# Delta-rule blocks of 16x16 inverted on VectorE, one block per partition, instead of by doublings on TensorE

## The reference

```python
def step(Sm, inp):
    q_, k_, v_, g_, b_ = inp
    Sm = Sm * jnp.exp(g_)[..., None, None]
    kv = jnp.einsum('bhk,bhkv->bhv', k_, Sm)
    delta = (v_ - kv) * b_[..., None]
    Sm = Sm + jnp.einsum('bhk,bhv->bhkv', k_, delta)
    o = jnp.einsum('bhk,bhkv->bhv', q_, Sm)
    return (Sm, o)
```

## Time and profile before

| | |
|---|---|
| median of three runs | 2876.7 us (2873.14 to 2880.99) |
| span of the profiled execution | 2973.8 us, mean TensorE clock 0.954 of full |
| PE, PEld busy | 2684.9 us (90%), 2275.1 us (77%) |
| DVE busy | 2384.7 us (80%) |
| ACT, POOL busy | 1828.3 us (61%), 1221.2 us (41%) |
| DMA | 153.27 MB, mean 52 GB/s |

### The profile page before, as it was taken

How to read it: one execution, slowest core, us unless ns; L and a number is a source line. 1 busy time by engine, 2 the same in 40 slices (tenths; PEclk the granted TensorE clock), 3 DMA queues, 4 the chain that set the end, 5 groups by cost and what they waited for, 6 DMA issues and landing times. The chain is left out here.

```text
span 2973.8 us, 122804 instructions
## 1 busy us (share of the span) xinstructions
PE 2684.9 (90%) x52271; PEld 2275.1 (77%) x52272; DVE 2384.7 (80%) x5006; ACT 1828.3 (61%) x5749; POOL 1221.2 (41%) x1048
## 2 busy tenths in 40 slices
PE   1478889999999999999999999999999999857898
PEld 1367668888888888888888888888888888724555
DVE  7556658888888888888888888888888888468796
ACT  1245546777777777777777777777777777501111
POOL 2456555343434343434343434343434343255420
PEclk7778889999999999999999999999999999978999
DMA  5221101111111111111111111111111110152311
GB/s 189 92 61 42 32 23 38 35 42 35 42 35 42 35 42 35 42 36 41 39 42 41 39 39 42 41 40 37 42 35 42 35 32 28 61 192 90 94 64 43
DMA packets 92834, 153.27 MB, mean 52 GB/s; under 512 B 16966, under 2 KB 60661, under 8 KB 91107
## 3 DMA queue, kind: packets, MB, share of 16 engines
q1 hardware_dynamic: 69491, 111.65, 12.9%
q0 software_dynamic: 12288, 24.19, 2.6%
q10 hardware_dynamic: 10512, 9.57, 0.9%
HBM read 114.38 MB, written 40.37 MB: 52 GB/s over the span
## 5 line engine op out<-in xcount | busy, mean ns | idle before, releaser
L1383 DVE SCALAR_TENSOR_TENSOR p_y<-p_xr,cw,p_y 128x512 f32<-128x512 f32 x768 | 652.2, 851 | 66.7 <-ACT p_y L1101 46.6
L740 PE MATMUL p_psF<-xnS,w_hl 128*128 128x512 f32 x1536 | 432.8, 417 | 24.1 <-PEq L628 11.1
L1655 POOL TENSOR_TENSOR p_Wr<-p_Ws,p_rho 128x512 f32<-128x512 f32 x96 | 135.8, 1436 | 651.0 <-ACT p_Ws L1198 651.0
L740 PEld LDWEIGHTS p_psF<-xnS,w_hl 128*128 128x128 f32 x1536 | 279.3, 195 | 87.3 <-issue 18.2
L1637 POOL TENSOR_TENSOR p_E<-p_E,p_sj 128x512 f32<-128x512 f32 x128 | 158.0, 1253 | 292.9 <-DVE p_sj L1409 292.9
L800 PEld LDWEIGHTS p_psI<-p_Dc,p_M 32*32 32x32 f32 x16384 | 180.1, 106 | 100.0 <-issue 91.9
L922 PE MATMUL p_psO<-p_wout,p_ont 128*128 128x256 f32 x1024 | 250.4, 399 | 0.7 <-ACT p_ont L1211 0.7
L800 PE MATMUL p_psI<-p_Dc,p_M 32*32 32x32 f32 x16384 | 215.7, 195 | 38.1 <-issue 33.7
L1678 POOL TENSOR_TENSOR p_O<-p_OG,p_sm 128x512 f32<-128x512 f32 x128 | 131.4, 1049 | 240.9 <-DVE p_sm L58 240.8
L1098 ACT ACTIVATE p_xr<-p_psF 128x512 f32<-128x512 f32 x256 | 154.1, 602 | 123.0 <-PE p_psF L740 119.8
L810 PEld LDWEIGHTS p_psI<-p_Xs,p_DTc 32*32 32x32 f32 x16384 | 168.5, 106 | 75.0 <-issue 70.0
(11 more groups left out here) (322 smaller groups left out, 6638.8 us busy)
## 6 DMA issues: line engine op xcount, KB each, us to landing
p_ab<-decays SPq DMA_DIRECT2D x64, 512.0 KB
w_raw<-in_w_in SPq DMA_DIRECT2D x16, 768.0 KB, 5.6
p_wgu<-in_w_gu SPq DMA_DIRECT2D x60, 176.0 KB
expert_out<-p_ye ACTq DMA_DIRECT2D x73, 128.0 KB, 1.8
expert_in<-p_zero SPq DMA_DIRECT2D x16, 512.0 KB, 7.1
p_xe<-expert_in SPq DMA_DIRECT2D x60, 128.0 KB
p_wd<-in_w_down SPq DMA_DIRECT2D x60, 88.0 KB
p_wout<-in_w_out SPq DMA_DIRECT2D x16, 256.0 KB
```

What stands on the lines that cost most here:

```text
L740: m = pe.matmul(b4(psF[f % 2][:, :]), w_hl[:, wp, kt, ty * P:(ty + 1) * P], xnS[:, xp, kt, :].rearrange("p (b t) -> p b t", b=B)[:, :, c * ...
L1383: m = dve.scalar_tensor_tensor(y[:, ty, :, :], xr[:, ty, :, tap:tap + P], cw[:, ty, tap:tap + 1], y[:, ty, :, :], ALU.mult, ALU.add)
```

## The change

Levels 1 to 3 and first_level go, with their passes on TensorE, copies on ScalarE and masks on GpSimd. Instead, compact(g) writes the 32 x 32 blocks with the opposite sign, SyncE stores them to DRAM (blocks_out), and gathers the 64 diagonal blocks of 16 x 16 (2 value heads, 4 batches, 8 blocks each) into U, one block in a partition as 256 elements. pivots(g) on VectorE inverts them in place: for each of the pivots 1 to 14 it multiplies the column above the pivot with the row to its right and adds the product. SyncE writes the blocks back to DRAM (blocks_back, whose other places hold zeros), and loads the 32 x 32 blocks into DTc, and turn_cores transposes them into Dc. From there level 4 goes on as before, with the one mask that it needs, and adds where it subtracted. pivots(g - 1) stands where the VectorE part of level 1 stood, turn_cores(g - 1) where level 3 stood. compact(g) moves on ScalarE ahead of squares(g, 1). SyncE's loads of a step are issued one step earlier in its program, between the transfers back and those out. Some semaphores and constants are merged.

```diff
+            def cores_out(g):
+                wait(sp, "compact", g, 4)
+                sp.dma_start(block_rows(blocks_out), ATc[:, :, :, :].rearrange("p v b t -> p (v b t)")).then_inc(apart, 16)
+                sp.wait_ge(apart, 16 * (g + 1))
+                for s_ in range(2):
+                    at = slice(s_ * CORES // 2, (s_ + 1) * CORES // 2)
+                    sp.dma_start(U[at, 0:CORE * CORE], core_rows(blocks_out, s_)).then_inc(gathered, 16)
+            def cores_back(g):
...
+                wait(sp, "pivoted", g, 1)
+                for s_ in range(2):
+                    at = slice(s_ * CORES // 2, (s_ + 1) * CORES // 2)
+                    sp.dma_start(core_rows(blocks_back, s_), U[at, 0:CORE * CORE]).then_inc(returned, 16)
+                sp.wait_ge(returned, 16 + 32 * (g + 1))
+                wait(sp, "spread", g - 2, 4)
+                sp.dma_start(DTc[g % 2][:, :, :, :].rearrange("p v b t -> p (v b t)"), block_rows(blocks_back)).then_inc(inverted, 16)
             def step(g):
-                decays_in(g)
-                unit_in(g)
-                head_in(g)
+                cores_back(g - 1)
+                loads(g + 1)
+                cores_out(g)
+                if g + 1 < STEPS:
+                    head_in(g + 1)
...
-                wait(act, "masked", g - 1, 2)
-                wait_event(act, "inverse_d", 1, g - 1)
+                wait(act, "masked", g - 1, 1)
+                if g:
+                    act.wait_ge(apart, 16 * g)
                 for q in range(4):
-                    act.activation(heads(ATc[quad(q), :, :, :]), heads(ATP[g % 2][quad(q), :, :, 0, quad(q)]), ACT.Copy).then_inc(s["compact"], 1)
+                    act.activation(heads(ATc[quad(q), :, :, :]), heads(ATP[g % 2][quad(q), :, :, 0, quad(q)]), ACT.Copy, scale=-1.0).then_inc(s["compact"], 1)
...
+            def pivots(g):
+                dve.wait_ge(gathered, 32 * (g + 1))
+                mark(dve.memset(diagonal, 1.0))
+                for k in range(1, CORE - 1):
+                    n = CORE - 1 - k
+                    rest, product = square[:, 0:k, k + 1:], pivot[:, 0:k * n].rearrange("p (i j) -> p i j", i=k)
+                    link(dve.tensor_tensor(product, square[:, 0:k, k:k + 1].to_broadcast([CORES, k, n]), square[:, k:k + 1, k + 1:].to_broadcast([CORES, k, n]), ALU.mult))
+                    m = dve.tensor_tensor(rest, rest, product, ALU.add)
+                    if k < CORE - 2:
+                        link(m)
+                m.then_inc(s["pivoted"], 1)
+            def turn_cores(g):
                 p = g % 2
                 wait(dve, "halved", g - 2, 2)
-                wait(dve, "spread", g - 2, 4)
                 wait_event(dve, "inverse_mm", "x5", g - 2)
-                wait(dve, "compact", g, 4)
-                link(dve.tensor_tensor(heads(Dc[p][:, :, :, :]), heads(ATc[:, :, :, :]), masks[:, 0, :].unsqueeze(1).to_broadcast([P, 2 * B, BLK]), ALU.mult))
-                link(dve.tensor_tensor(heads(DTc[p][:, :, :, :]), identc[:, :].unsqueeze(1).to_broadcast([P, 2 * B, BLK]), heads(Dc[p][:, :, :, :]), ALU.subtract))
+                dve.wait_ge(inverted, 16 * (g + 1))
                 dve.transpose(heads(Dc[p][:, :, :, :]), heads(DTc[p][:, :, :, :])).then_inc(s["inverse_d"], 1)
...
                 if g >= 1:
-                    level(g - 1, 1)
+                    pivots(g - 1)
```

More of the change, by code:

```diff
@@ L370, in link @@
                 ch.wait()
-            pool.memset(zero[:, :], 0.0).then_inc(zero_set, 1)
+            ch.then(pool.memset(zero[:, :], 0.0))
             pool.wait_ge(consts_loaded, 16 * n_consts)
@@ L434, with heads_and_experts @@
 H = P // 2
-def heads_and_experts(nc, A, R, adram, xnbuf, xbuf, ybuf):
+def heads_and_experts(nc, A, R, adram, blocks_out, blocks_back, xnbuf, xbuf, ybuf):
     xnS, ident, acc, put_u, gates = R["xnS"], R["ident"], R["acc"], R["put_u"], R["gates"]
@@ L1271, in step @@
                     out_squares(g - 2, 1)
+                compact(g)
                 squares(g, 1)
@@ L1444, in level @@
                 wait_event(dve, "inverse_mm", f"y{l}", g)
-                link(dve.tensor_tensor(D_, D_, vb(psI[g % 2][:, 256:512]), ALU.subtract))
+                link(dve.tensor_tensor(D_, D_, vb(psI[g % 2][:, 256:512]), ALU.add))
                 dve.transpose(heads(DTc[g % 2][:, :, :, :]), D_).then_inc(s["inverse_d"], 1)
@@ L1563, in step @@
                 if g >= 1:
-                    level(g - 1, 3)
+                    turn_cores(g - 1)
                 if g >= 2:
@@ L1595, in _ @@
             history(STEPS - 1, 0)
-            level(STEPS - 1, 1)
+            pivots(STEPS - 1)
             gather_out(STEPS - 3)
@@ L1600, in _ @@
             level6(STEPS - 2)
-            level(STEPS - 1, 2)
             history(STEPS - 1, 1)
             outputs(STEPS - 2, 0)
-            level(STEPS - 1, 3)
+            turn_cores(STEPS - 1)
             outputs(STEPS - 2, 1)
@@ L1728, in step @@
                     normed(g - 2)
-                mask(g, 0)
+                mask(g)
                 scatter(g, 11)
@@ L1740, in _ @@
                 step(g)
-            mask(STEPS - 1, 1)
             rho_w(STEPS - 2)
@@ L2338, in build_program @@
     adram = nc.dram_tensor("decays", (HV, NC, B, P), F32, kind="Internal").ap()
+    blocks_out = nc.dram_tensor("blocks_out", (BLK, 2 * B * P // BLK, BLK), F32, kind="Internal").ap()
+    blocks_back = nc.dram_tensor("blocks_back", (BLK, 2 * B * P // BLK, BLK), F32, kind="Internal").ap()
     xnbuf = nc.dram_tensor("tokens_in", (B * S, D), F32, kind="Internal").ap()
```

118 lines of the change are left out of this document (55 added, 63 removed).

## The result

The changed kernel takes 3001.82 us (median of four runs, 3000.6 to 3007.45), against 2878.64 before: ratio 1.0432, 95% interval 1.0416 to 1.0449. It is 123 us slower; forecast were 2942 us and slower. The profiled execution has a span of 3000.6 us.

What follows compares the result with a forecast made beforehand. TensorE was taken to set the pace, VectorE next and setting it after the change. 14 heads x 6.4 = 90, less 25 for the first heads, gave +65 on 2876.7: 2942 us, range 2855 to 3045.

Steps and rivals of the forecast that it cites:

- rival (c): TensorE's holes lower its clock; matmuls on the chain at half speed a third of it, about 1 us a step: 3000; chance 0.08.
- (b): Way back through DRAM late, 16 us instead of 10; turn_cores holds VectorE 3 us net every step: 3110; chance 0.16.
- their price: Pivots on VectorE: 28 linked instructions, 6.6 us a step, from a fixed 0.205 us each plus 1.1 ns an element.
- Rival (a): Pivot instructions cost less than the 12-element rows; at 0.15 us each, 4.2 us a step: 2807 us; chance 0.16.
- The dense steps: Steps lengthen by 3.2, 0.8, 0.8 and 1.6 us in chunks 0 to 3; 6.4 a head, 14 heads: 90 us.
- compact's 1.72 us ahead of the query squares: ScalarE's four copies between output and query squares lengthen the chain from solve to L1502 from 11.9 to 13.6 us.
- the forecast's sums: Solve's start on TensorE after the step's scan: 13.95 us in chunk 3 (was 11.54), 15.9 in chunk 0 (was 11.04).
- TensorE's wait at turn_keys: Sign expected in the profile after: TensorE waits at turn_keys for ScalarE's silu, which it did not do before.
- The first two heads: Eight steps gain 25 us net, from VectorE's 67.8 us of waits for y passes between 140 and 460 us.
- Rival (d): First heads give back nearly all of 67.8 us, GpSimd's lighter load 0.4 us a step: 2880, no change; chance 0.12.
- The transfers: DRAM hops hidden: 15 us for two hops out and gather; way back 7 to 10 us against 9.5 of cover.
- The tail: After the dense part, the levels' ping-pong and the round trip are about equal: 0.

Runs made afterwards that it cites:

- the repeated products: Changed kernel with TensorE's level6_x products done twice more in chunks 1 and 3, five times more in chunk 0, ahead of its gather_out wait: 2974.40 us, ratio 1.0333.
- the second one: The kernel before, unchanged, profiled once more: span 2878.0 us.
- both moves: Changed kernel with gather_out ahead of the pivots and compact back behind the expert's gate: 2860.53 us, ratio 0.9942 to the kernel before.

## Why the prediction was right, and which terms were mis-sized

**The direction and its ground held.** TensorE lost its work and stopped being the bound; the pivots on VectorE lie on the path, up to four fifths of them by the run with half of them. The time came out 60 us above the forecast; it is inside the range by the room that the range left for rival (c) and a part of (b). Of their price, forecast from the earlier trace rows, the slope and the fixed part were right: in the trace after, a pivot instruction of 14 elements takes 0.17 and one of 56 elements 0.21:

```profile
1614.59 0.21 DVE L1464 TENSOR_TENSOR p_pivot<-p_U 64x56 f32<-64x56 f32 x1
...
1618.05 0.17 DVE L1465 TENSOR_TENSOR p_U<-p_U,p_pivot 64x14 f32<-64x14 f32 x1
```

By the Trainium skill (VectorE: DVE Perf Modes, the section on the TRN2 errata) the (N + 151)/0.96 ns would be 172 and 216 ns, the other term, 58 cycles plus N, 75 and 119, all estimates; the trace agrees with the first. Rival (a) falls with it.

**The dense steps: +90 forecast, +121 measured.** Of the forecast step, compact's 1.72 us ahead of the query squares was right: taking it back gave 1.7 a step. Chunks 1 and 2 came out a little better (+0.8 each forecast, +0.6 and +0.2 measured), chunk 3 worse (+1.6 forecast, +2.7), and chunk 0 holds nearly all of what is missing (+3.2 forecast, +5.4). The step that failed is the clock, which the prediction left at 1.00, and ahead of it the wait that brings it down. The prediction named as waiting behind the pivots ScalarE, then TensorE's turn_keys and solve. It counted gather_out among the work behind the pivots, but not who waits for gather_out: queries_state, which stands in TensorE's order ahead of a projection, a transposition and level6_y. Where the clock stays at 1.00 behind this wait, the solve starts at 14.05 in chunk 3 and, with the repeated products, at 16.10 in chunk 0; the forecast's sums were 13.95 and 15.9. Steps with these solves last 40.2 us in either chunk, +1.9 and +3.2. Where the clock falls, the solve starts at 15.6 in chunk 3 and at 17.8 to 18.6 in chunk 0. That 13.95 and 14.05 agree so closely is partly luck: VectorE's work, which the prediction added up, ends with level 6 at 13.48, and the solve then still waits for TensorE's own work behind queries_state, 5.4 us from 8.64 on. TensorE's wait at turn_keys, which the prediction gave as a sign, is small in the changed kernel (28.5 us in 12); it comes in nearly every step once gather_out stands in front (102.8 us in 47).

**The clock: forecast 1.00, measured 0.94.** Rival (c) named the cause of what is missing in the dense part: with the holes filled by work that changes nothing, the 55 steps lose 83 us against the kernel before, where the forecast's terms by chunk make 88 for them. The price of the low clock is at least these 38 us, where (c) reckoned 56. That its 3000 is so near to the measured time is luck, since it also carries the 25 us of the first heads that did not come. Moving gather_out gave 36, but it takes away the wait and the low clock behind it together, so the two do not add. The prediction gave this rival 0.08 because its holes were under 2 us each; in chunk 3 a wait of 2.0 to 2.2 us was followed by the low clock in six steps and not in seven, and in chunk 0 the wait was 4.7 to 6.9.

**The first two heads: -25 forecast, -1.5 measured.** The 67.8 us of the earlier trace rows came from an execution 96 us longer than the second one, and 75 of them lie in the steps 1 to 7 (343.5 against 268.8 us). The prediction carried the difference over unscaled, but drew one term from the very stretch in which that execution was unusual. Rival (d) falls with this term.

**The transfers: hidden, as forecast.** The way back takes 6.1 to 8.2 us where its length can be read (forecast 7 to 10). From the end of the pivots to turn_cores there are 9.7 to 13.7 us in the 55 steps, where 9.5 was forecast. A hop more changed nothing; rival (b) falls. The gap is there to be used up: in the kernel with divided pivots turn_cores waits. From SyncE's queue, in the first of the two chunk-3 steps above:

```profile
1618.25 0.84 SPq L724 DMA_DIRECT2D blocks_back<-p_U  x2
1620.50 0.55 SPq L727 DMA_DIRECT2D p_DTc<-blocks_back  x1
...
1638.79 0.52 SPq L709 DMA_DIRECT2D blocks_out<-p_ATc  x1
1642.06 1.95 SPq L713 DMA_DIRECT2D p_U<-blocks_out  x2
```

L727 and L713 wait for the transfer before them, so the store of 64-byte pieces has landed at the latest 2.25 us after its issue, where 2.6 to 5.6 plus 1.8 was reckoned: its 1024 packets take 10 ns each in the trace, and not the 41 to 88 ns of the mean packet. The store of 128 KB to blocks_out has landed at the latest 3.27 us after, where expert_out, of the same size, lands in 1.7. The Trainium skill's rule (DMA: Bandwidth & Descriptors, on why a DMA increments its semaphore by 16), by which blocks_out, seen as 4 x 32 x 256, uses 4 engines, fits this: 1.6 us more at most, against an estimate of 1. So do its packets, all that the core moved from 1638.7 to 1642:

```profile
DMA packets 132, 0.13 MB, mean 40 GB/s; under 512 B 4, under 2 KB 132, under 8 KB 132
```

The 128 of 1 KB take 55 ns each and lie between 1639.95 and 1641.71, four at a time in the mean; four small ones end them, where 32 end the two stores of 64-byte pieces.

**The tail: 0 forecast, +2.9 measured.**

What stays open: why the same wait of TensorE is followed by the low clock in some steps and not in others, what of the pivots' four fifths is the clock's, and why the sum of both moves is 7 us more than their gains apart, which is little more than the spread of the runs. Pivots between the outputs and the squares, where VectorE still has idle time, were not tried; that asks for another order of level 4 on all engines.

## What to carry to other kernels

When work is put at the head of an engine's step, follow every result that this engine makes behind it, not only the chain in mind: here an accumulation of 1.2 us that came late held up TensorE, whose clock then fell (38 us over the dense part), and a copy of 1.7 us placed on the chain cost 98. Work at such a place may also lie beside a wait for data that is not ready yet, and moving it away brings that wait out (200 us here). A term that is read from a stretch in which the profiled execution is unlike the median wants a second profile before it is counted. A single step read in order of time can be of one of two kinds, as the two chunk-3 steps above are, so count the kinds over all steps before a term is judged by one.

## What the runs showed of the hardware

A wait of 2.01 us on TensorE was followed by a granted clock of 0.71, 0.50 and 0.94 in the next three windows of 2 us in one chunk-3 step, and by 1.00 throughout in the next chunk-3 step. Doing the same products twice more in that wait kept the clock at 1.00 at this place in all 27 steps of chunks 1 and 3 and, with five more in chunk 0, made the kernel 27 us faster. In the kernel with both moves the same remedy gave 9 us, net of 0.8 us a step that too many repeats cost in chunk 0.
